# All high parts of g made by VectorE from PSUM, with w_y's parts ahead and w_out's and b_out's parts in the gate stage

## The chip, the cores and the metric

The kernel runs on one core of one Trainium2 chip, in one launch. The metric is the device time of that core in microseconds (us), the median of the runs that are shown. Each core has five engines that run side by side and meet only at semaphores: PE (TensorE, matrix multiply; its weight loads have a row of their own, PEld), DVE (VectorE), ACT (ScalarE), POOL (GpSimd) and SP (SyncE, here only the issuer of DMAs). Each takes its instructions strictly in the order in which the program wrote them. Matmuls read SBUF and write PSUM; DVE and ACT reach both; POOL works on SBUF alone.

## The reference

The input x has 2 sequences of 512 tokens and 256 channels. It is normalised per token (xn) and goes into two branches, whose outputs are added to x:

```
recurrent branch                                  feed-forward branch
y  = gelu(xn @ w_y + b_y)                         w1q, w3q, w2q = ternary(w) * mean|w|
conv = 4-tap causal conv of (xn @ w_x + b_x)      h1 = xn @ w1q.T ; h3 = xn @ w3q.T     (682 wide)
gate_x = sigmoid(conv @ w_ig + b_ig)              g  = silu(h1) * h3
gate_a = sigmoid(conv @ w_ag + b_ag)              out += g @ w2q.T
a  = exp(-8 gate_a softplus(a_param))
h_t = a_t h_(t-1) + gate_x conv sqrt(1 - a^2)     (a scan over the 512 tokens)
out += (h * y) @ w_out + b_out
```

All data is float32. The kernel multiplies in TensorE's rounded float32 type and keeps accuracy by splitting: an operand v becomes a high part (v rounded to that type) and a low part (v minus its high part), and a product of two such operands is three matmuls (high-high, high-low, low-high). A ternary weight is exact in the type, so a product with it needs only the two parts of the other operand.

## The kernel before

Channels lie on the 128 partitions, in KC = 2 chunks, and tokens along the free axis, 512 per sequence, so that nearly every elementwise instruction is 128x512. The order of work is written out by hand, engine by engine: the body of each `@block` is that engine's queue, and semaphores (`wait_ge`, `then_inc`) tie the queues together. PSUM is four slots of two banks, `slot[0]` to `slot[3]`, passed from stage to stage.

The stages, as PE sees them:

- **Start.** x is normalised on DVE (`statistics`, `variance`, `normalise`; the reciprocal root on POOL, `rstd_of`), transposed on PE, and split into `xt_hi` (ACT) and `xt_lo` (DVE). Weights are split too: `square_hi(m)` rounds one 256x256 matrix to `w_hi`, `square_lo(m)` makes `w_lo` on POOL. The matrices are WX, WY, WIG, WAG and WOUT.
- **Gate stage.** x @ w_x, x @ w_y, the convolution (`older_taps` on DVE), its parts `conv_hi` (ACT, L420) and `conv_lo` (POOL, `lo_of_conv`, L290), the products with w_ig and w_ag, then tanh and exp on ACT. `conv_lo(s, c)` of sequence s and chunk c is read by `gate_product` on PE. While this runs, DVE makes w1 and w3 ternary (`ternary_13`: two instructions `below`, L563, then two that write `w13_q`, L566) and after that w2 (`ternary_w2`, L604 and L606). PE's `sums_of_w13` has to be done before the first of these, and the first hidden tile needs both halves of `w13_q` and the scales that `threshold_2` makes (L571 to L576).
- **Hidden stage.** Ten tiles of 128 hidden channels by 512 tokens, `hidden(0)` to `hidden(9)`, eight matmuls each, put h1 into one bank and h3 into the other bank of one of slots 0 to 2. ACT makes `silu` of h1 (`silu_of`, L404); DVE multiplies by h3, which it reads from PSUM, into `g` (`g_of`, L616); ACT copies g into the high part `g_hi` (`g_hi_of`, L410; POOL does the last one, L329); POOL subtracts to the low part `g_lo` (`lo_of_g`, L295). silu and g have rings of three buffers. `hidden(n)` from n = 3 on waits until the g of the tile three before it has been made, since it uses that slot again. The last 42 channels go through `hidden_tail`, `tail_product` (L669), `tail_hi` and `tail_lo` (L676).
- **Scan and output.** `down(0)` and `down(1)` multiply g's parts with ternary w2, while the recurrence runs on the side: the square root on ACT (`mult_of`, L451, with a table load ahead of it), then on DVE `gated_products` (L638), `scan` (L649) and `gated_output` (L655) four times in a row, hy_hi on ACT (L457) and hy_lo on POOL (L346). `project(s, ...)` multiplies with w_out's parts (L812), and DVE adds x (`output`, L662). b_out rides in two extra rows of w2: its parts `b_split` are copied into `w2_q` by two small DMAs from SP, which wait for both.

In this kernel w_out's parts and b_split are made in the hidden stage: POOL waits for the squares of a (`a2_set`) and then makes both parts of w_out, ahead of its first `lo_of_g`; b_out's high part stands in ACT's queue after `g_hi_of(4)`, its low part in POOL's after the fifth `lo_of_g`. The two pads of the tail buffer gt (`gt_pads`, L286) stand between POOL's `lo_of_conv`.

## Time and profile before

| What | Value |
|---|---|
| three runs | 74.97, 74.77 and 74.32 us, median 74.77 |
| the profiled execution | 74.64 us, of which the profile's span covers 72.8 us |
| granted TensorE clock | 1.0 of full speed in every slice |
| PE busy | 68.1 us, 93% of the span |
| PEld busy | 58.9 us, 81% |
| DVE busy | 56.8 us, 78% |
| ACT busy | 52.5 us, 72% |
| POOL busy | 47.4 us, 65% |
| chain that ended last | PE 41%, DVE 17%, POOL 13%, issue 11%, ACT 9% of the span |

Busy shares are averages over stages that have different limits: a share tells which engine has much to do, not which one the end waits for. For that one reads, stage by stage, which wait ended last ahead of an instruction. Numbers on a time line are us from the start of the span. An instruction's row starts where its engine took it up; if it then had to wait for something that no semaphore shows, the wait is inside its duration, and it is seen by comparing with the same instruction elsewhere.

### The profile page before, as it was taken

The numbers are of one execution on the slowest core, as the hardware profiler recorded it, in microseconds if no ns is written. First come the engines' busy times: TensorE is split into PE (matmuls) and PEld (weight loads), VectorE is DVE, ScalarE is ACT, GpSimd is POOL, SyncE is SP. The second block draws the span as 40 slices with busy tenths as digits, with TensorE's granted clock in tenths as the row PEclk, the third lists the DMA queues.
The fourth block names the chain that finished last, engine by engine and source line by source line (L and its number), as shares of the span: only waits on it lengthen the run. The fifth ranks groups of instructions, "written<-read, shape, count | busy, mean of one in ns | idle before, by whom it ended". The sixth has DMA issues, their size and how long they took to land.

```text
span 72.8 us, 1128 instructions
## 1 busy us (share of the span) xinstructions
PE 68.1 (93%) x378; PEld 58.9 (81%) x378; DVE 56.8 (78%) x93; ACT 52.5 (72%) x81; POOL 47.4 (65%) x64
## 2 busy tenths in 40 slices
...
GB/s 6 230 295 332 361 377 395 382 99 0 9 0 0 4 0 0 0 0 0 0 0 9 0 0 9 0 0 0 1 0 0 0 0 0 9 0 0 200 193 183
DMA packets 5112, 5.63 MB, mean 77 GB/s; under 512 B 541, under 2 KB 4594, under 8 KB 5106
## 3 DMA queue, kind: packets, MB, share of 16 engines
...
## 4 chain that ended last, share of the span: by engine, by line
PE 41%; DVE 17%; POOL 13%; issue 11%; ACT 9%; DMA 3%; POOLq 2%; DVEq 0%; ACTq 0%
PE slot L753 21%; PE slot L770 10%; DVE slot L649 5%; PE slot L876 4%; DVE w_raw L616 4%; ACT w_raw L404 4%; POOL rstd L263 4%; DMA par<-params 3%; POOL w_lo L247 3%; PE slot L812 3%; PE slot L779 3%; DVE gt L676 2%; DVE xn_y L544 2%; DVE slot L638 2%; POOLq L52 2%
## 5 line engine op out<-in xcount | busy, mean ns | idle before, releaser
L295 POOL TENSOR_TENSOR g_lo<-w_raw,g_hi 128x512 fp32r<-128x512 f32 x10 | 14.7, 1488 | 2.3 <-ACT g_hi L410 2.2
L770 PE MATMUL slot<-xt_hi,w_q 128*128 128x512 f32 x40 | 15.8, 396 | 0.4 <-DVE w_raw L616 0.4
L770 PE MATMUL slot<-xt_lo,w_q 128*128 128x512 f32 x40 | 15.7, 393 | 0.0
L616 DVE SCALAR_TENSOR_TENSOR w_raw<-w_raw,s,slot 128x512 f32<-128x512 f32 x10 | 7.2, 746 | 5.2 <-ACT w_raw L404 5.2
L802 PE MATMUL slot<-w_q,g_lo 128*128 128x256 f32 x40 | 9.7, 283 | 0.0
L802 PE MATMUL slot<-w_q,g_hi 128*128 128x256 f32 x40 | 9.7, 283 | 0.0
L770 PEld LDWEIGHTS slot<-xt_hi,w_q 128*128 128x128 f32 x40 | 7.5, 188 | 2.6 <-DVE w_raw L616 1.0
L594 DVE SCALAR_TENSOR_TENSOR conv<-slot,par,conv 128x511 f32<-128x511 f32 (+2 forms) x12 | 9.0, 748 | 0.4
L770 PEld LDWEIGHTS slot<-xt_lo,w_q 128*128 128x128 f32 x40 | 7.5, 188 | 1.7
L242 POOL CAST w_hi<-w_raw 128x512 fp32r<-128x512 f32 x3 | 1.8, 614 | 9.7 <-DVE mult L628 9.7
L410 ACT ACTIVATE g_hi<-w_raw 128x512 fp32r<-128x512 f32 x9 | 5.7, 629 | 3.2 <-DVE w_raw L616 3.2
L802 PEld LDWEIGHTS slot<-w_q,g_lo 128*128 128x128 f32 x40 | 7.7, 192 | 0.0
L802 PEld LDWEIGHTS slot<-w_q,g_hi 128*128 128x128 f32 x40 | 7.7, 191 | 0.0
L247 POOL TENSOR_TENSOR w_lo<-w_raw,w_hi 128x512 fp32r<-128x512 f32 (+1 forms) x6 | 6.6, 1106 | 1.3 <-DVE xn_y L544 0.8
L404 ACT ACTIVATE w_raw<-slot,scale 128x512 f32<-128x512 f32 x10 | 6.6, 679 | 0.2
L346 POOL TENSOR_TENSOR conv_lo<-tx,conv_hi 128x512 fp32r<-128x512 f32 x4 | 5.1, 1284 | 2.3 <-ACT conv_hi L457 2.3
L819 PE MATMUL slot<-ones 128*128 128x128 f32 (+1 forms) x26 | 5.7, 408 | 1.0 <-POOL ones L230 1.0
L819 PEld LDWEIGHTS slot<-ones 128*128 128x128 f32 x26 | 5.5, 319 | 1.0 <-POOL ones L230 1.0
L457 ACT ACTIVATE conv_hi<-tx 128x512 fp32r<-128x512 f32 x4 | 2.5, 632 | 4.7 <-DVE tx L655 4.7
L290 POOL TENSOR_TENSOR conv_lo<-conv,conv_hi 128x512 fp32r<-128x512 f32 x4 | 5.7, 1420 | 0.2
L534 DVE BATCH_NORM_STATS2 stats<-x_sb 128x6 f32<-128x256 f32 x8 | 3.1, 413 | 2.3 <-DMA x_sb<-x 2.3
L753 PE MATMUL slot<-conv_hi,w_hi 128*128 128x512 f32 x12 | 4.7, 395 | 0.0
...
## 6 DMA issues: line engine op xcount, KB each, us to landing
...
```

Source lines behind the costliest of these rows:

```text
L247: nc.gpsimd.tensor_tensor(w_lo[:, m, c], w_raw[:, m, c], w_hi[:, m, c].bitcast(f32), ALU.subtract).then_inc(w_lo_set, len(chunks))
L290: nc.gpsimd.tensor_tensor(conv_lo[:, s, c], conv[:, s, c], conv_hi[:, s, c].bitcast(f32), ALU.subtract).then_inc(conv_lo_set, 1)
L295: nc.gpsimd.tensor_tensor(g_lo[:, j, s], g[:, n % RING], g_hi[:, j, s].bitcast(f32), ALU.subtract).then_inc(g_lo_set, 1)
L346: nc.gpsimd.tensor_tensor(hy_lo[:, s, c], tx[:, s, c], hy_hi[:, s, c].bitcast(f32), ALU.subtract).then_inc(hy_lo_set, 1)
L404: nc.scalar.activation(silu[:, n % RING], slot[H_SLOT[s][j]][:, 0], ACT.Silu, scale=scale[:, 0:1]).then_inc(silu_set, 1)
L410: nc.scalar.activation(g_hi[:, j, s], g[:, n % RING], ACT.Copy).then_inc(g_hi_set, 1)
L594: nc.vector.scalar_tensor_tensor(out=conv[:, s, c, i:], in0=slot[X_SLOT[s]][:, c, 0:SEQ - i], scalar=par[:, CONV_W + KC * k + c:CONV_W + K ...
L616: nc.vector.scalar_tensor_tensor(out=g[:, n % RING], in0=silu[:, n % RING], scalar=s32[:, 0:1], in1=slot[H_SLOT[s][j]][:, 1], op0=ALU.mult ...
L753: mm = nc.tensor.matmul(dst[:, o], w[:, m, c, o * P:(o + 1) * P], v[:, c], start=(first and i == 0 and c == 0), stop=(last and i == len(te ...
L770: mm = nc.tensor.matmul(slot[H_SLOT[s][j]][:, o], w13_q[:, c, col:col + P], v[:, s, c], start=(c == 0 and v is xt_hi), stop=(c == KC - 1 a ...
L802: nc.tensor.matmul(out_tile(s, i, t), v[:, s, rows], w2_q[:, j], start=(j == 0 and t == tiles.start and k == 0), stop=False, skip_group_ch ...
L819: nc.tensor.matmul(slot[WARM_SLOT][:, 0, 0:cols], ones[:, :], ones[:, 0:cols], start=True, stop=True)
```

## The change

Five edits go together.

- **g's high parts.** `g_hi_of(n)` moves from ACT (nine) and POOL (one) to DVE. It no longer rounds the stored g: it computes silu * s32 * h3 a second time from PSUM, with the output in the rounded type. It stands right behind `g_of(n)`. ACT's `silu_of` and PE's `hidden` now wait for `g_hi_set`, not `g_set`, since the second instruction reads the same buffers.
- **w_y.** ACT makes w_y's high part ahead of the Gelu table load; POOL makes the first half of its low part ahead of the second sequence's `rstd_of`. On PE, w_y's product is split so that the transposes of the second sequence stand between its terms, and on DVE one `statistics` of the second sequence stands between the two `xt_lo` of the first.
- **w_out.** Its high part goes to ACT behind `conv_hi_of(0, 0)`, its low part to POOL behind `lo_of_conv(0, 1)`, with semaphores of their own.
- **b_out.** The high part goes to ACT behind `gelu_of(0)`, the low part to POOL between `lo_of_conv(1, 0)` and `lo_of_conv(1, 1)`.
- **Pads and order.** One pad of gt goes to POOL's start, the other behind `lo_of_conv(0, 0)`. POOL's `half_biases` and `rates` come later. DVE's `gated_input(1)` moves from behind `g_of(1)` to ahead of `ternary_w2`, and `tail_lo` goes one tile later.

```diff
 POOL, at its start
+            nc.gpsimd.memset(gt[32:HALF].bitcast(f32), 1.0).then_inc(gt_pads_set, 1)
...
 POOL, start and gate stage
             square_lo(WX)
+            square_lo(WY, range(0, 1))
             rstd_of(1, slice(0, TILES // 2), 3)
             rstd_of(1, slice(TILES // 2, TILES), 4)
             pool.wait_ge(xn_set, 2 * TILES)
-            for c in range(KC):
-                square_lo(WY, range(c, c + 1))
+            square_lo(WY, range(1, KC))
             for m in (WIG, WAG):
                 square_hi(m)
                 square_lo(m)
             lo_of_conv(0, 0)
+            pool.wait_ge(conv_lo_set, 1)
+            nc.gpsimd.memset(gt[96:P].bitcast(f32), 0.0).then_inc(gt_pads_set, 1)
+            pool.wait_ge(gt_pads_set, 2)
+            lo_of_conv(0, 1)
+            pool.wait_ge(wout_hi_set, 1)
+            nc.gpsimd.tensor_tensor(w_lo[:, WOUT], w_raw[:, WOUT], w_hi[:, WOUT].bitcast(f32), ALU.subtract).then_inc(wout_lo_set, 1)
             half_biases()
             rates()
-            lo_of_conv(0, 1)
-            gt_pads(slice(32, HALF), 1.0, KC)
-            pool.wait_ge(gt_pads_set, 1)
             lo_of_conv(1, 0)
-            gt_pads(slice(96, P), 0.0, KC + 1)
-            pool.wait_ge(gt_pads_set, 2)
+            pool.wait_ge(b_hi_set, 1)
+            nc.gpsimd.tensor_tensor(b_split[:, 1], b_row[:, :], b_split[:, 0].bitcast(f32), ALU.subtract).then_inc(b_split_set, 1)
             lo_of_conv(1, 1)
-            pool.wait_ge(a2_set, SEQS)
-            square_hi(WOUT)
-            square_lo(WOUT)
             for n in range(2 * FULL):
-                if n == 2 * FULL - 1:
-                    pool.wait_ge(g_set, n + 1)
-                    nc.gpsimd.tensor_copy(g_hi[:, HJ[n][1], HJ[n][0]], g[:, n % RING]).then_inc(g_hi_set, 1)
                 lo_of_g(n)
...
 ACT
             xt_hi_of(0)
+            square_hi(WY)
             act.wait_ge(quarter_set, 2)
             nc.scalar.activation(gelu_in[:, 1:2], gelu_in[:, 0:1], ACT.Gelu)
-            square_hi(WY)
...
             conv_hi_of(0, 0)
+            act.wait_ge(w_loaded[WOUT], 16)
+            nc.scalar.activation(w_hi[:, WOUT], w_raw[:, WOUT], ACT.Copy).then_inc(wout_hi_set, 1)
             newest_tap(1)
             conv_hi_of(0, 1)
             gelu_of(0)
+            act.wait_ge(b_out_loaded, 16)
+            nc.scalar.activation(b_split[:, 0], b_row[:, :], ACT.Copy).then_inc(b_hi_set, 1)
...
-                    act.wait_ge(g_set, n - RING + 1)
+                    act.wait_ge(g_hi_set, n - RING + 1)
...
-            g_hi_of(0)
...
+            for n in range(2, 2 * FULL):
                 silu_of(n)
-                if n > FULL:
-                    g_hi_of(n - 1)
-                if n == FULL + 1:
+                if n == FULL - 1:
+                    tail_hi(gt_hi[HALF:HALF + TAIL])
+                if n == FULL + 2:
                     tail_hi(gt[0:TAIL])
...
 DVE
+            def g_hi_of(n):
+                s, j = HJ[n]
+                nc.vector.scalar_tensor_tensor(out=g_hi[:, j, s], in0=silu[:, n % RING], scalar=s32[:, 0:1],
+                                               in1=slot[H_SLOT[s][j]][:, 1], op0=ALU.mult, op1=ALU.mult).then_inc(g_hi_set, 1)
...
             gated_input(0)
+            gated_input(1)
             ternary_w2()
             squares(0)
             squares(1)
-            g_of(0)
-            g_of(1)
-            gated_input(1)
+            for n in range(2):
+                g_of(n)
+                g_hi_of(n)
             tail_product()
...
 PE
-            dense_terms(slot[Y_SLOT[0]], WY, [(w_hi, xt_hi[:, 0]), (w_hi, xt_lo[:, 0])], True, False)
+            dense_terms(slot[Y_SLOT[0]], WY, [(w_hi, xt_hi[:, 0])], True, False)
             transposes(1, first_half)
+            dense_terms(slot[Y_SLOT[0]], WY, [(w_hi, xt_lo[:, 0])], False, False)
             transposes(1, second_half)
...
             hidden(2)
-            pe.wait_ge(g_set, 1)
+            pe.wait_ge(g_hi_set, 1)
             hidden(3)
...
-            pe.wait_ge(w_lo_set, KC * (WOUT + 1))
+            pe.wait_ge(wout_lo_set, 1)
             project(0, range(len(O_TILES[0])))
```

POOL's queue in the gate stage, before (w_lo is a weight's low part, half_b to a_rate are the small constants, gt the tail's pads; the semaphores that an instruction waits for stand in brackets):

```order
L290 TENSOR_TENSOR conv_lo<-conv,conv_hi 128x512 [waits conv_hi_set]
L281 TENSOR_SCALAR half_b<-par 128x4
L252 TENSOR_SCALAR sp_e<-par 128x2 [waits sp_log]
L254 TENSOR_TENSOR sp_e<-sp_e 128x2 [waits rate_set]
L256 TENSOR_SCALAR a_rate<-sp_e 128x2 [waits rate_set]
L290 TENSOR_TENSOR conv_lo<-conv,conv_hi 128x512 [waits conv_hi_set]
L286 MEMSET gt 32x1024 [waits conv_lo_set]
L290 TENSOR_TENSOR conv_lo<-conv,conv_hi 128x512 [waits conv_hi_set,gt_pads_set]
L286 MEMSET gt 32x1024 [waits conv_lo_set]
L290 TENSOR_TENSOR conv_lo<-conv,conv_hi 128x512 [waits conv_hi_set,gt_pads_set]
L242 CAST w_hi<-w_raw 128x512 [waits w_loaded4,a2_set]
L247 TENSOR_TENSOR w_lo<-w_raw,w_hi 128x512 [waits w_hi_set]
```

The same stretch now:

```order
L293 TENSOR_TENSOR conv_lo<-conv,conv_hi 128x512 [waits conv_hi_set]
L318 MEMSET gt 32x1024 [waits conv_lo_set]
L293 TENSOR_TENSOR conv_lo<-conv,conv_hi 128x512 [waits conv_hi_set,gt_pads_set]
L322 TENSOR_TENSOR w_lo<-w_raw,w_hi 128x512 [waits wout_hi_set]
L289 TENSOR_SCALAR half_b<-par 128x4
L260 TENSOR_SCALAR sp_e<-par 128x2 [waits sp_log]
L262 TENSOR_TENSOR sp_e<-sp_e 128x2 [waits rate_set]
L264 TENSOR_SCALAR a_rate<-sp_e 128x2 [waits rate_set]
L293 TENSOR_TENSOR conv_lo<-conv,conv_hi 128x512 [waits conv_hi_set]
L327 TENSOR_TENSOR b_split<-b_row,b_split 1x256 [waits b_hi_set]
L293 TENSOR_TENSOR conv_lo<-conv,conv_hi 128x512 [waits conv_hi_set]
```

Between the second and the third conv_lo there are now w_out's low part and the four small instructions, where one pad stood; between the third and the fourth b_split stands in place of the other pad.

DVE's queue from the second sequence's gated input to the third g, before (tx is the gated input, mult the squares; w_raw with slot among its inputs is g, and with below the tail's product):

```order
L622 SCALAR_TENSOR_TENSOR tx<-tx,conv 128x1024 [waits tx_set]
L604 TENSOR_SCALAR below<-w_raw,thr 128x1536 [waits w13_q_set,s2_ready]
L606 SCALAR_TENSOR_TENSOR w_q<-w_raw,thr,below 128x1536 [waits below_set]
L628 TENSOR_TENSOR mult<-ta 128x2x511 [waits a_set] x2
L616 SCALAR_TENSOR_TENSOR w_raw<-w_raw,s,slot 128x512 [waits silu_set,scale2_set]
L616 SCALAR_TENSOR_TENSOR w_raw<-w_raw,s,slot 128x512 [waits silu_set]
L622 SCALAR_TENSOR_TENSOR tx<-tx,conv 128x1024 [waits tx_set]
L669 SCALAR_TENSOR_TENSOR w_raw<-below,s,slot 42x1024 [waits silu_t_set]
L616 SCALAR_TENSOR_TENSOR w_raw<-w_raw,s,slot 128x512 [waits silu_set]
```

The same stretch now:

```order
L612 SCALAR_TENSOR_TENSOR tx<-tx,conv 128x1024 [waits tx_set] x2
L588 TENSOR_SCALAR below<-w_raw,thr 128x1536 [waits w13_q_set,s2_ready]
L590 SCALAR_TENSOR_TENSOR w_q<-w_raw,thr,below 128x1536 [waits below_set]
L618 TENSOR_TENSOR mult<-ta 128x2x511 [waits a_set] x2
L600 SCALAR_TENSOR_TENSOR w_raw<-w_raw,s,slot 128x512 [waits silu_set,scale2_set]
L606 SCALAR_TENSOR_TENSOR g_hi<-w_raw,s,slot 128x512
L600 SCALAR_TENSOR_TENSOR w_raw<-w_raw,s,slot 128x512 [waits silu_set]
L606 SCALAR_TENSOR_TENSOR g_hi<-w_raw,s,slot 128x512
L659 SCALAR_TENSOR_TENSOR w_raw<-below,s,slot 42x1024 [waits silu_t_set]
L600 SCALAR_TENSOR_TENSOR w_raw<-w_raw,s,slot 128x512 [waits silu_set]
L606 SCALAR_TENSOR_TENSOR g_hi<-w_raw,s,slot 128x512
```

Both gated inputs stand ahead of the first g, and each g is followed by its g_hi, so that the first g_hi is the seventh instruction behind the first gated input.

## Rows read from the trace of the kernel before

**Rows 1.** Time line, PE: start, duration, engine, line, operation, out<-in, shape, count, idle time before.

```profile
32.10 0.39 PE L770 MATMUL slot<-xt_hi,w_q 128*128 128x512 f32 x1
...
39.49 0.39 PE L770 MATMUL slot<-xt_hi,w_q 128*128 128x512 f32 x1
...
49.30 0.50 PE L770 MATMUL slot<-xt_hi,w_q 128*128 128x512 f32 x1 [0.39 <-DVE w_raw L616]
...
53.10 0.28 PE L802 MATMUL slot<-w_q,g_hi 128*128 128x256 f32 x1
...
67.44 0.40 PE L812 MATMUL slot<-w_lo,conv_hi 128*128 128x256 f32 x2
```

**Rows 2.** The chain of waits, its end: start, duration, what.

```profile
68.30 1.94 PE slot L812 x14
```

**Rows 3.** Time line, POOL: the last low part of hy.

```profile
66.97 1.27 POOL L346 TENSOR_TENSOR conv_lo<-tx,conv_hi 128x512 fp32r<-128x512 f32 x1 [0.64 <-ACT conv_hi L457]
```

**Rows 4.** Time line, DVE: the first gated product.

```profile
56.94 0.70 DVE L638 TENSOR_TENSOR slot<-tx,slot 128x512 f32<-128x512 f32 x1 [1.19 <-ACT slot L451]
```

**Rows 5.** Time line, ACT: the last silu.

```profile
54.16 0.67 ACT L404 ACTIVATE w_raw<-slot,scale 128x512 f32<-128x512 f32 x1
```

**Rows 6.** Time line, DVE, from 24 us to the tail.

```profile
24.14 2.77 DVE L563 TENSOR_SCALAR below<-w_raw,thr 128x1408 bf16<-128x1408 f32 x2
...
31.47 1.21 DVE L622 SCALAR_TENSOR_TENSOR tx<-tx,conv 128x1024 f32<-128x1024 f32 x1
32.60 1.01 DVE L604 TENSOR_SCALAR below<-w_raw,thr 128x1536 bf16<-128x1536 f32 x1
...
37.65 1.41 DVE L616 SCALAR_TENSOR_TENSOR w_raw<-w_raw,s,slot 128x512 f32<-128x512 f32 x2
38.96 1.97 DVE L622 SCALAR_TENSOR_TENSOR tx<-tx,conv 128x1024 f32<-128x1024 f32 x1
40.97 1.29 DVE L669 SCALAR_TENSOR_TENSOR w_raw<-below,s,slot 42x1024 f32<-42x1024 f32 x1
...
46.31 2.16 DVE L676 TENSOR_TENSOR gt<-w_raw,gt_hi 42x1024 fp32r<-42x1024 f32 x1
```

**Rows 7.** Groups by line and shape, DVE's ternary instructions: busy us, mean ns, idle before.

```profile
L566 DVE SCALAR_TENSOR_TENSOR w_q<-w_raw,thr,below 128x1408 fp32r<-128x1408 f32 x1 | 2.7, 2705 | 0.0
L563 DVE TENSOR_SCALAR below<-w_raw,thr 128x1364 bf16<-128x1364 f32 x1 | 1.7, 1698 | 0.0
L566 DVE SCALAR_TENSOR_TENSOR w_q<-w_raw,thr,below 128x1364 fp32r<-128x1364 f32 x1 | 1.6, 1627 | 0.0
L563 DVE TENSOR_SCALAR below<-w_raw,thr 128x1408 bf16<-128x1408 f32 x1 | 1.1, 1146 | 0.0
```

**Rows 8.** Time line, ACT: the last tap and conv_hi(0, 1) in the gate stage.

```profile
18.05 1.44 ACT L389 ACTIVATE conv<-slot,conv_c,par 128x509 f32<-128x509 f32 x2 [0.62 <-PE slot L753]
19.38 0.63 ACT L420 ACTIVATE conv_hi<-conv 128x512 fp32r<-128x512 f32 x1
```

**Rows 9.** Time line, POOL, the second rstd and the gate stage.

```profile
10.12 0.22 POOL L260 TENSOR_SCALAR v_eps<-mv 128x2 f32<-128x2 f32 x1 [1.40 <-DVE mv L539]
...
19.76 0.24 POOL L281 TENSOR_SCALAR half_b<-par 128x4 f32<-128x4 f32 x1
...
20.86 1.30 POOL L290 TENSOR_TENSOR conv_lo<-conv,conv_hi 128x512 fp32r<-128x512 f32 x1
22.22 0.95 POOL L286 MEMSET gt<- 32x1024 f32 x1
23.25 1.29 POOL L290 TENSOR_TENSOR conv_lo<-conv,conv_hi 128x512 fp32r<-128x512 f32 x1
24.60 1.58 POOL L286 MEMSET gt<- 32x1024 f32 x1
26.26 1.79 POOL L290 TENSOR_TENSOR conv_lo<-conv,conv_hi 128x512 fp32r<-128x512 f32 x1
```

**Rows 10.** Groups by line and shape, POOL: b_out's low part.

```profile
L333 POOL TENSOR_TENSOR b_split<-b_row,b_split 1x256 fp32r<-1x256 f32 x1 | 0.7, 728 | 0.0
```

More of the change, by code:

```diff
@@ L182, in build @@
         o_psum, o_set = sem("o_psum"), sem("o_set")
+        LAST = 2 * FULL - 2
         HJ = [(s, j) for s in range(SEQS) for j in range(FULL)]
@@ L402, in silu_of @@
                 if n >= RING:
-                    act.wait_ge(g_set, n - RING + 1)
+                    act.wait_ge(g_hi_set, n - RING + 1)
                 nc.scalar.activation(silu[:, n % RING], slot[H_SLOT[s][j]][:, 0], ACT.Silu,
                                      scale=scale[:, 0:1]).then_inc(silu_set, 1)
-            def g_hi_of(n):
-                s, j = HJ[n]
-                act.wait_ge(g_set, n + 1)
-                nc.scalar.activation(g_hi[:, j, s], g[:, n % RING], ACT.Copy).then_inc(g_hi_set, 1)
             def tail_hi(dst):
@@ L494, in _ @@
                                  scale=scale[0:TAIL, 0:1]).then_inc(silu_t_set, 1)
-            g_hi_of(1)
-            silu_of(2)
-            silu_of(3)
-            g_hi_of(2)
-            tail_hi(gt_hi[HALF:HALF + TAIL])
-            silu_of(4)
-            g_hi_of(3)
-            g_hi_of(4)
-            act.wait_ge(b_out_loaded, 16)
-            nc.scalar.activation(b_split[:, 0], b_row[:, :], ACT.Copy).then_inc(b_hi_set, 1)
-            for n in range(FULL, 2 * FULL - 1):
+            for n in range(2, 2 * FULL):
                 silu_of(n)
-                if n > FULL:
-                    g_hi_of(n - 1)
-                if n == FULL + 1:
+                if n == FULL - 1:
+                    tail_hi(gt_hi[HALF:HALF + TAIL])
+                if n == FULL + 2:
                     tail_hi(gt[0:TAIL])
-            g_hi_of(2 * FULL - 2)
-            silu_of(2 * FULL - 1)
             for s in range(SEQS):
@@ L545, in normalise, with xt_lo_of @@
                                             ALU.subtract, ALU.mult).then_inc(xn_set, 1)
-            def xt_lo_of(s):
-                for h in range(2):
+            def xt_lo_of(s, parts=range(2)):
+                for h in parts:
                     dve.wait_ge(xt_hi_set, 2 * s + h + 1)
@@ L687, in _ @@
                 normalise(0, tile_halves[i], i + 1)
-            xt_lo_of(0)
-            for i in range(2):
-                dve.wait_ge(x_loaded[TILES + i], 16)
-                statistics(1, tile_halves[i])
-                variance(1, tile_halves[i])
+            xt_lo_of(0, [0])
+            dve.wait_ge(x_loaded[TILES], 16)
+            statistics(1, [0])
+            xt_lo_of(0, [1])
+            statistics(1, [1])
+            variance(1, tile_halves[0])
+            dve.wait_ge(x_loaded[TILES + 1], 16)
+            statistics(1, tile_halves[1])
+            variance(1, tile_halves[1])
             normalise(1, tile_halves[0], 3)
@@ L709, in _ @@
             squares(1)
-            g_of(0)
-            g_of(1)
-            gated_input(1)
+            for n in range(2):
+                g_of(n)
+                g_hi_of(n)
             tail_product()
-            g_of(2)
-            g_of(3)
-            g_of(4)
-            tail_lo()
-            for n in range(FULL, 2 * FULL - 1):
-                g_of(n)
-            dve.wait_ge(g_set, 9)
-            first_root(0, 0)
-            g_of(9)
-            dve.wait_ge(g_set, 10)
-            first_root(0, 1)
+            for n in range(2, LAST):
+                g_of(n)
+                g_hi_of(n)
+                if n == FULL:
+                    tail_lo()
+            for n in range(LAST, 2 * FULL):
+                g_of(n)
+                g_hi_of(n)
+                dve.wait_ge(g_hi_set, n + 1)
+                first_root(0, n - LAST)
             for s in range(SEQS):
```

36 lines of the change are left out of this document (18 added, 18 removed).

## The prediction, made before the changed kernel was run

> **What bounds the kernel now.** I read the engines' busy shares, then the chain of waits from its end, then the time lines of the engines it runs through, stage by stage. The profiled execution took 74.64 us, 0.13 under the median of the runs (74.77); all sums are made against it.
>
> The chain's last step is 1.94 us of PE from 68.30 [rows 2], and that start is where two strands meet. One is PE itself. Its hidden stage runs from 32.10 to 53.10 at (39.49 - 32.10) / 4 = 1.85 us per tile of eight matmuls (the tail's eight count as a tile), 0.23 each, with one wait ahead of hidden(8) [rows 1]: that starts at 49.30 where 1.85 a tile allows 39.49 + 5 x 1.85 = 48.74, and its first matmul takes 0.50 instead of 0.39, so about 0.65 is lost there. From 53.10, which I call H, PE goes without a gap until the two matmuls at 67.44, which at 0.12 each free it at 67.68 [rows 1]: 14.58 us from H. The other strand begins with the last silu, silu(9), at 54.16 [rows 5], goes through the root to DVE's first gated product, which waited 1.19 for ACT [rows 4], and through scans, hy_hi and hy_lo to 66.97 + 1.27 = 68.24 [rows 3]. That is 14.08 from silu(9). PE stands 0.62 waiting for it. So H may rise by 0.6 before PE alone is late, provided that silu(9) does not rise too; it starts 1.06 behind H now, because ACT's copies of g stand ahead of it, and a hand-over needs only about 0.22 (a matmul's row lasts 0.39 and the next starts after 0.23, so 0.16, and 0.06 from hy_lo's end to PE's start) [rows 1 to 3, 5].
>
> Ahead of the hidden stage DVE is the engine to watch. From 24.14 to 31.08 it makes w1 and w3 ternary [rows 6], while POOL works at conv_lo and pads [rows 9]. There the same instruction takes very different times [rows 7]. `below` on w2, undisturbed, takes 1.01 for 1536 elements [rows 6], so 0.93 and 0.90 are due for 1408 and 1364; it took 1146 and 1698 ns. w_q took 1627 ns for 1364, so 1.68 is due for 1408; it took 2705 ns. Losses: 0.2, 0.8 and 1.0. In the same stretch POOL's second pad took 1.58 instead of 0.95 and the last conv_lo 1.79 instead of 1.29 [rows 9]. The two engines take turns here.
>
> **The change, part by part.** *POOL's gate stage.* conv_lo(0, 1) cannot start before conv_hi(0, 1) ends at 19.38 + 0.63 = 20.0 [rows 8]. Then follow 1.30 for it, 1.30 for w_out's low part (priced by conv_lo, the same subtraction and shape) and 1.10 for half_biases and rates (20.86 - 19.76): conv_lo(1, 0) starts at 23.7 where it started at 23.25, and ends at 25.0 [rows 9]. DVE, ready at about 24.1 [rows 6], stands until then. After that the turns are 0.93 `below`, 0.73 b_split [rows 10], 0.90 `below`, 1.29 conv_lo(1, 1), 1.68 and 1.63 w_q: 25.0 + 7.16 = 32.2. Neighbouring rows of an engine overlap by 0.08 (24.14 + 2.77 against 26.83 [rows 6]), 0.4 over five joints, so 31.8, against 31.08: +0.7.
>
> The unknown is b_split, on one partition. No row shows such an instruction in DVE's way, so it costs DVE between 0 and 0.73. I take 0.73, because the nearest row, a pad on 32 of 128 partitions, cost `below` the 0.8 above. By the Trainium skill ("SBUF — State Buffer", section "Who interferes with whom") the engine that issues first holds the shared ports for its whole instruction and the other one fully blocks; by that, width does not count, the 0.73 stands and the result is the forecast's, while without it DVE would be 0.73 earlier and the second rival below would hold.
>
> *DVE up to the first g_hi.* Before, g(0) starts at 37.65 [rows 6]. Now it comes 0.7 later, and another 1.13 later for gated_input(1), which is moved ahead of it (32.60 - 31.47): 39.5. g and g_hi are 0.70 each (1.41 for two), so g_hi(0) ends at 40.9 [rows 6]. g_hi is priced as g, from which it differs only in its output type.
>
> *PE up to hidden(3).* hidden(0) needs DVE's scales, which end 0.4 behind w13_q [rows 6], at 32.1 or 32.2, and it needs the gate products, whose last 14 matmuls at 0.23 follow conv_lo(1, 1) at about 28.8: 32.0. So it starts where it did, at 32.1, whatever w_y's new place gains PE before. hidden(3), ready at 39.49, now waits for g_hi(0) until 40.95: +1.45 on PE.
>
> *The rest of the hidden stage.* A pair costs DVE 1.4 against PE's 1.85 per tile, so DVE catches up. tail_product (1.29 [rows 6]) stands between the second and third pair: g_hi(2) ends at 40.9 + 1.4 + 1.3 + 1.4 less joints, 44.85, where hidden(5) is ready at 40.95 + 2 x 1.85 = 44.65: +0.25. The 0.65 lost ahead of hidden(8) had tail_lo (2.16 at 46.31 [rows 6]) ahead of g(5); that now stands behind g_hi(5), which ends at 48.9, with hidden(8) ready at 50.45: -0.65. tail_lo then ends at 51.1 at its old length, g_hi(6) at 52.4, and hidden(9) is ready at 52.3: +0.1. H = 53.10 + 1.45 + 0.25 - 0.65 + 0.1 = 54.25.
>
> *The end.* PE frees itself at 54.25 + 14.58 = 68.83. silu(9) has no copies ahead of it and starts at H + 0.22 = 54.47, so hy_lo ends at 68.55, and PE no longer waits for it. 68.83 instead of 68.30 is 0.53, less 0.1 for a first matmul that no longer follows a wait: +0.45. Result 74.64 + 0.45 = 75.1.
>
> *At nothing.* ACT loses nine copies and POOL two casts and one subtraction in the hidden stage; neither is late there but for silu(9), already counted. The first pad at POOL's start lies in its wait for the parameters, and the half of w_y's low part, 0.7, in the 1.40 that it is idle at 10.12 [rows 9]. w_out's high part on ACT, 0.63 like conv_hi, fits the idle 0.62 ahead of the last tap [rows 8]; were that gone, conv_hi(0, 1) and all of POOL's stretch would come 0.6 later, which is the first rival's case. b_out's high part stands ahead of conv_hi(1, 0), with POOL's use of it at 23.7, two microseconds later. SP's two b_split DMAs come earlier and have only stores behind them. On PE's start the transposes move between w_y's terms; what that gains ends at the wait for the scales.
>
> **Rivals.** *POOL comes too late (slower).* If POOL reaches conv_lo(1, 0) after DVE has begun `below`, about 24.0, the turns change: `below` to 24.95, conv_lo(1, 0) to 26.25, `below`, b_split to 27.9, w_q to 29.6, and only then conv_lo(1, 1), to 30.9. The gate products then let hidden(0) start at about 34.1, hidden(3) at 41.5, and H is 54.8: +1.0, 75.6. It decides at a delay of 0.3 on POOL between 20.0 and 23.7; for it speaks that POOL waits for ACT twice there, against it that w_out's high part is done long before. Chance 0.22.
>
> *b_split does not hold DVE (faster).* DVE is 0.73 earlier from the first `below` on, hidden(3) waits 0.7, H is 53.5, silu(9)'s strand ends at 67.8 and PE at 68.1: -0.3, 74.3. Is POOL also 0.4 quicker up to conv_lo(1, 0) than summed, and hence DVE, it is 73.9. For it speaks that one partition is little, against it the pad's 1.58 and DVE's 1698 ns [rows 7, 9]. Chance 0.25.
>
> *DVE becomes the bound of the hidden stage.* If g_hi costs more than g, or tail_lo and the pairs are disturbed by POOL's g_lo, H slips by 0.5 more: 75.6. Against it: 1.4 against 1.85 a tile. Chance 0.08.
>
> **How the numbers follow.** The forecast, 75.1, has 0.45; its own range is 74.7 to 75.5, from the joints and hand-overs that I rounded. The range of 73.9 to 75.8 takes in the first two rivals but for their outer ends. One per cent, 0.75 us, is about what a measurement of this kernel can tell from no change. Faster than 74.0 takes the better half of the second rival and a tenth for what I have not seen, mostly at PE's start: 0.22. Slower than 75.5 takes most of the first, the third and a tenth of the forecast: 0.27. Within: 0.51.
>
> **What would show it.** A wait of DVE's about 0.9 inside the first `below` (some 1.8 instead of 1146 ns), a second `below` of about 1.6 and a first w_q of 2.9; PE waiting 1.4 for g_hi ahead of hidden(3) and not ahead of hidden(8); silu(9) within 0.3 of H; no wait of PE's for hy_lo at the end. I am wrong if conv_lo(1, 1) ends past 30, if hidden(3) starts before 40.3, or if PE's last wait is still for hy_lo.

## The result, and the profile of the changed kernel

| Timing | before | changed | ratio (95% interval) |
|---|---|---|---|
| first, 4 runs each | 74.56 us | 75.38 us | 1.0096 (1.0058 to 1.0134) |
| again, 12 runs beside 23 of before | 74.67 us | 74.97 us | 1.0046 (1.0026 to 1.0066) |

The changed kernel is slower, by 0.8 us in the first timing and by 0.3 us in the second. The forecast was 75.1, +0.45. Executions of one kernel also differ ahead of the gate stage: DVE's first `below` starts at 24.38 and at 23.98 in two profiles of the changed kernel, and at 24.14 before [rows 6]. So the profiles are compared from this start on, and in the changed kernel the rows are those of the execution with 24.38. From there PE's last matmuls end 46.10 later before (68.30 + 1.94 [rows 2]) and 46.52 later now: **+0.42**. The rows follow; each answers to rows of before.

Time line of DVE in the changed kernel, from w13's ternary instructions to the tail:

```profile
24.38 4.38 DVE L547 TENSOR_SCALAR below<-w_raw,thr 128x1408 bf16<-128x1408 f32 x2
28.68 3.22 DVE L550 SCALAR_TENSOR_TENSOR w_q<-w_raw,thr,below 128x1408 fp32r<-128x1408 f32 x2
...
32.28 2.35 DVE L612 SCALAR_TENSOR_TENSOR tx<-tx,conv 128x1024 f32<-128x1024 f32 x2
...
39.60 0.74 DVE L600 SCALAR_TENSOR_TENSOR w_raw<-w_raw,s,slot 128x512 f32<-128x512 f32 x1
40.26 0.74 DVE L606 SCALAR_TENSOR_TENSOR g_hi<-w_raw,s,slot 128x512 fp32r<-128x512 f32 x1
...
41.58 0.74 DVE L606 SCALAR_TENSOR_TENSOR g_hi<-w_raw,s,slot 128x512 fp32r<-128x512 f32 x1
...
44.33 0.74 DVE L606 SCALAR_TENSOR_TENSOR g_hi<-w_raw,s,slot 128x512 fp32r<-128x512 f32 x1
...
49.44 1.22 DVE L666 TENSOR_TENSOR gt<-w_raw,gt_hi 42x1024 fp32r<-42x1024 f32 x1
```

The first g_hi ends at 41.00 (forecast 40.9). Three things put it there, and all are in the rows: w1 and w3 are ternary at 31.90, 7.52 after the first `below`, where it was 6.94 [rows 6]; two gated inputs stand ahead of w2 (2.35) where one stood (1.21); and g_hi itself takes 0.66 from start to start, as g does, so it was priced right.

Time line of PE, at hidden(0), hidden(3), hidden(5) and H (the first matmul of the down stage):

```profile
32.44 0.47 PE L764 MATMUL slot<-xt_hi,w_q 128*128 128x512 f32 x1 [0.24 <-DVE thr L557]
...
41.05 0.50 PE L764 MATMUL slot<-xt_hi,w_q 128*128 128x512 f32 x1 [0.99 <-DVE g_hi L606]
...
45.13 0.50 PE L764 MATMUL slot<-xt_hi,w_q 128*128 128x512 f32 x1
...
54.49 0.28 PE L796 MATMUL slot<-w_q,g_hi 128*128 128x256 f32 x1
```

The wait ahead of hidden(8) [rows 1] is gone, and one ahead of hidden(3) is there. A small one stands at hidden(5), which starts 0.28 after the 44.85 that the tile before it allows; the view does not mark it. H is 30.11 after the first `below`, before it was 28.96: +1.15, as the terms of the forecast sum to.

The chain of waits of the changed kernel, its end (start, duration, what):

```profile
45.13 9.52 PE slot L764 x40
54.65 10.54 PE slot L796 x88
65.19 5.71 PE slot L806 x48
70.93 0.42 DVE x_sb L652
```

From hidden(5) on the chain is PE alone: no wait for hy_lo, which stood at 68.30 before [rows 2]. ACT's last silu and POOL's last hy_lo, from their time lines:

```profile
54.69 0.69 ACT L402 ACTIVATE w_raw<-slot,scale 128x512 f32<-128x512 f32 x1 [1.16 <-PE slot L764]
```

```profile
67.51 1.30 POOL L344 TENSOR_TENSOR conv_lo<-tx,conv_hi 128x512 fp32r<-128x512 f32 x1 [0.64 <-ACT conv_hi L450]
```

The last silu is 0.20 behind H (before 1.06 [rows 1, 5]); hy_lo ends at 68.81, 0.26 ahead of the matmul that reads it (54.49 + 14.58 = 69.07). The 0.6 that PE used to wait at the end paid for half of the later H.

Time line of POOL, from the start to the hidden stage, and DVE's ternary groups (busy us, mean ns):

```profile
9.57 0.74 POOL L255 TENSOR_TENSOR w_lo<-w_raw,w_hi 128x256 fp32r<-128x256 f32 x1 [1.04 <-ACT w_hi L353]
...
19.33 0.95 POOL L318 MEMSET gt<- 32x1024 f32 x1
20.39 1.29 POOL L293 TENSOR_TENSOR conv_lo<-conv,conv_hi 128x512 fp32r<-128x512 f32 x1
21.65 1.29 POOL L322 TENSOR_TENSOR w_lo<-w_raw,w_hi 128x512 fp32r<-128x512 f32 x1
23.02 0.25 POOL L289 TENSOR_SCALAR half_b<-par 128x4 f32<-128x4 f32 x1
...
24.14 1.30 POOL L293 TENSOR_TENSOR conv_lo<-conv,conv_hi 128x512 fp32r<-128x512 f32 x1
25.38 1.39 POOL L327 TENSOR_TENSOR b_split<-b_row,b_split 1x256 fp32r<-1x256 f32 x1
26.74 1.29 POOL L293 TENSOR_TENSOR conv_lo<-conv,conv_hi 128x512 fp32r<-128x512 f32 x1
41.08 2.62 POOL L298 TENSOR_TENSOR g_lo<-w_raw,g_hi 128x512 fp32r<-128x512 f32 x2 [13.05 <-DVE g_hi L606]
...
49.49 2.33 POOL L298 TENSOR_TENSOR g_lo<-w_raw,g_hi 128x512 fp32r<-128x512 f32 x1 [0.40 <-DVE g_hi L606]
```

```profile
L547 DVE TENSOR_SCALAR below<-w_raw,thr 128x1364 bf16<-128x1364 f32 x1 | 2.7, 2655 | 0.0
...
L547 DVE TENSOR_SCALAR below<-w_raw,thr 128x1408 bf16<-128x1408 f32 x1 | 1.8, 1802 | 0.0
L550 DVE SCALAR_TENSOR_TENSOR w_q<-w_raw,thr,below 128x1408 fp32r<-128x1408 f32 x1 | 1.7, 1672 | 0.0
```

Against the undisturbed times, 0.93 and 0.90, DVE lost 0.87 in the first `below` and 1.75 in the second, 2.6 in all (before 2.0 [rows 7]). conv_lo(1, 0) came 0.24 ahead of the first `below`: that narrow was the margin. In the hidden stage g_hi takes its 0.74 also beside POOL's g_lo (41.58, while two g_lo run from 41.08 to 43.70), and tail_lo, taken up at 49.44, comes 0.05 ahead of a g_lo: here it is POOL that loses, 2.33 for 1.3.

### The profile page after: what moved, and what is told of

It is laid out like the page before. It is cut to its first block, busy times and chain, and to the rows that moved or that the text cites. A ratio compares the mean times of both kernels' runs of the same rounds, so it can differ in the third digit from the quotient of the medians.

```text
span 73.6 us, 1128 instructions
## 1 busy us (share of the span) xinstructions
PE 68.4 (93%) x378; PEld 59.0 (80%) x378; DVE 62.0 (84%) x103; ACT 48.2 (66%) x73; POOL 44.9 (61%) x62
## 4 chain that ended last, share of the span: by engine, by line
PE 48%; DVE 38%; issue 8%; ACT 2%; POOL 0%; DVEq 0%; ACTq 0%; POOLq 0%
PE slot L796 14%; PE slot L764 13%; DVE conv L578 10%; PE slot L806 8%; PE slot L813 7%; DVE below L547 6%; PE slot L838 4%; DVE mult L618 3%; DVE tx L612 3%; DVE g_hi L606 3%; DVE w_q L550 2%; DVE w_raw L600 2%; DVE w_q L590 2%; DVE xt_lo L534 2%; DVE below L588 1%
## 5 line engine op out<-in xcount | busy, mean ns | idle before, releaser
L298 POOL TENSOR_TENSOR g_lo<-w_raw,g_hi 128x512 fp32r<-128x512 f32 x10 | 14.0, 1401 | 16.2 <-DVE g_hi L606 16.1
L606 DVE SCALAR_TENSOR_TENSOR g_hi<-w_raw,s,slot 128x512 fp32r<-128x512 f32 x10 | 7.4, 742 | 0.0
L255 POOL TENSOR_TENSOR w_lo<-w_raw,w_hi 128x512 fp32r<-128x512 f32 (+1 forms) x5 | 5.4, 1071 | 2.4 <-ACT w_hi L353 1.0
L293 POOL TENSOR_TENSOR conv_lo<-conv,conv_hi 128x512 fp32r<-128x512 f32 x4 | 5.2, 1291 | 0.2
L747 PE MATMUL slot<-conv_hi,w_lo 128*128 128x512 f32 x12 | 4.7, 393 | 0.0
```

The source lines that it names most:

```text
L255: nc.gpsimd.tensor_tensor(w_lo[:, m, c], w_raw[:, m, c], w_hi[:, m, c].bitcast(f32), ALU.subtract).then_inc(w_lo_set, len(chunks))
L293: nc.gpsimd.tensor_tensor(conv_lo[:, s, c], conv[:, s, c], conv_hi[:, s, c].bitcast(f32), ALU.subtract).then_inc(conv_lo_set, 1)
L298: nc.gpsimd.tensor_tensor(g_lo[:, j, s], g[:, n % RING], g_hi[:, j, s].bitcast(f32), ALU.subtract).then_inc(g_lo_set, 1)
L606: nc.vector.scalar_tensor_tensor(out=g_hi[:, j, s], in0=silu[:, n % RING], scalar=s32[:, 0:1], in1=slot[H_SLOT[s][j]][:, 1], op0=ALU.mult, ...
L747: mm = nc.tensor.matmul(dst[:, o], w[:, m, c, o * P:(o + 1) * P], v[:, c], start=(first and i == 0 and c == 0), stop=(last and i == len(te ...
```

## The experiments

The theory: what was lost is lateness in DVE's queue up to the third g_hi, made of turns that POOL takes, of gated_input(1) and of the pairs of g and g_hi; PE is late by what they are late. Rivals: the ten pairs set the hidden stage's end whatever stands ahead; b_split does not hold DVE; the start is to blame. Every ratio below is against runs of the kernel before, taken beside it. The new places of the two pads were not tried by themselves.

**The changed kernel again**, unaltered, as the measure for the others:

> The changed kernel once more, unaltered, as a measure for the others of this group: its first timing rests on four runs (ratio 1.0096, 1.0058 to 1.0134), and the profiles of the variants start up to 0.3 us apart, by when x arrives. All theories: 1.006 to 1.012.

Measured 1.0046 (1.0026 to 1.0066), just under what all theories gave, with an interval that reaches into it. Its profile has the same waits, 0.4 earlier throughout: from the first `below` on, H (30.11) and PE's end (46.52) are the same to the hundredth. The kernels below are set beside this second timing. Expectations written ahead of it went by the first, 1.0096, and so lie about 0.005 too high.

**b_out's low part back in the loop of g_lo.**

```diff
 lo_of_conv(1, 0)
-b_split on POOL
 lo_of_conv(1, 1)
 for n in range(2 * FULL):
     lo_of_g(n)
+    if n == FULL - 1: b_split on POOL
```

> The changed kernel with one thing undone: b_out's low part (b_split on POOL, one partition) stands behind the fifth lo_of_g again, no longer between the last two lo_of_conv. Theory (all that is lost is lateness of DVE's queue up to the first g_hi, and PE is late by the same amount): the second 'below' took 2655 ns beside b_split and conv_lo; without b_split's 0.73 it takes about 1.9, the first g_hi ends 0.7 earlier (40.3 for 41.0), hidden(3) starts at 40.3, the hidden stage ends at 53.8 for 54.49, and the time falls by 0.7, to that of the kernel before (ratio 1.000). Rival A (ten pairs of g and g_hi on DVE set the hidden stage's end, whatever stands ahead): hidden(3) starts earlier, but later tiles wait and the time stays at ratio 1.009. Rival B (one partition does not hold DVE): the second 'below' keeps its 2.6 us, because conv_lo comes at once.

Measured 1.0099 (1.0064 to 1.0134): the gain did not come, but not for the reason that rival A has. Time lines of this kernel, DVE, PE and POOL:

```profile
24.30 3.67 DVE L548 TENSOR_SCALAR below<-w_raw,thr 128x1408 bf16<-128x1408 f32 x2
...
48.65 2.67 DVE L667 TENSOR_TENSOR gt<-w_raw,gt_hi 42x1024 fp32r<-42x1024 f32 x1
```

```profile
40.27 0.51 PE L765 MATMUL slot<-xt_hi,w_q 128*128 128x512 f32 x1 [0.76 <-DVE g_hi L607]
52.81 0.50 PE L765 MATMUL slot<-xt_hi,w_q 128*128 128x512 f32 x1 [0.80 <-DVE g_hi L607]
```

```profile
48.25 0.73 POOL L331 TENSOR_TENSOR b_split<-b_row,b_split 1x256 fp32r<-1x256 f32 x1
48.95 1.28 POOL L298 TENSOR_TENSOR g_lo<-w_raw,g_hi 128x512 fp32r<-128x512 f32 x1
```

The two `below` took 3.67 for 4.38, so b_split had cost DVE 0.71 of its 0.73, on one partition: rival B falls. hidden(3) started 0.78 earlier (0.70 counted from the first `below`). In its new place b_split stood beside tail_lo, which asked at 48.65, was kept out by b_split and by g_lo(5) behind it, and took 2.67 for 1.22; hidden(9) then waited 0.80. The loss had moved, and it had grown: H is 30.46 after the first `below`, for 30.11 in the changed kernel.

**w_out's low part behind the squares.**

```diff
 lo_of_conv(0, 1)
-pool.wait_ge(wout_hi_set, 1); w_out's low part
 half_biases(); rates()
 lo_of_conv(1, 0); b_split; lo_of_conv(1, 1)
+pool.wait_ge(a2_set, SEQS); pool.wait_ge(wout_hi_set, 1); w_out's low part
```

> The changed kernel with w_out's low part on POOL behind the last lo_of_conv, where it waits for the squares of a (about 39.7 us) instead of standing ahead of half_biases. Theory (DVE's queue): POOL reaches conv_lo(1, 0) 1.3 earlier, at 22.8 for 24.14, so it is over before DVE's first 'below' (24.38). b_split then holds that 'below' for about 0.5 in place of the 0.87 lost now, and conv_lo(1, 1), which waits for conv_hi(1, 1) until 25.3, holds the second for 1.2 in place of 1.75. The first g_hi ends about 0.9 earlier, the time falls by 0.9: ratio 0.998. w_out's low part then runs beside g and g_hi, which read PSUM, and disturbs nothing. Rival A (the pairs): ratio stays 1.009. Rival C (each conflict avoided comes back with the next instruction of POOL): the first g_hi ends less than 0.3 earlier.

Measured 0.9879 (0.9858 to 0.9900), 1.7% below the changed kernel's second timing, more than expected. DVE's groups of this kernel:

```profile
L548 DVE TENSOR_SCALAR below<-w_raw,thr 128x1364 bf16<-128x1364 f32 x1 | 2.0, 1965 | 0.0
...
L548 DVE TENSOR_SCALAR below<-w_raw,thr 128x1408 bf16<-128x1408 f32 x1 | 1.2, 1244 | 0.0
```

The two `below` lost 0.31 and 1.06, 1.37 for 2.62: 1.25 less, where I had counted 0.9. PE's last matmuls end 45.27 after the first `below`, for 46.52: 1.25 less, too, and the time fell by as much (1.67% of 74.77). What DVE gained there arrived in full at the end.

**gated_input(1), in two other places.**

```diff
-gated_input(0); gated_input(1); ternary_w2()
+gated_input(0); ternary_w2()
 ...
+gated_input(1)      # first kernel: behind the second pair; second kernel: behind the seventh
```

> The changed kernel with gated_input(1) behind the second pair of g and g_hi, where the kernel before has it, instead of ahead of w2's ternary instructions. Theory: the first g_hi ends 1.13 earlier, at 39.9, and hidden(3) starts at 39.95 for 41.05; but gated_input(1) and the tail's product now both stand ahead of the third pair, g_hi(2) ends at 45.1 as it does now, hidden(5), ready at 43.6, waits 1.4, and the time is unchanged: ratio 1.009, between 1.006 and 1.012. Rival (only the first g_hi counts): the time falls by 1.0, ratio 0.996.

Measured 1.0036 (1.0018 to 1.0055), unchanged within the intervals. hidden(3) did not wait; PE's wait stood two tiles later, and PE ends 46.54 after the first `below`, for 46.52. Time lines of DVE, gated_input(1), and of PE:

```profile
40.92 1.22 DVE L612 SCALAR_TENSOR_TENSOR tx<-tx,conv 128x1024 f32<-128x1024 f32 x1
```

```profile
44.96 0.50 PE L764 MATMUL slot<-xt_hi,w_q 128*128 128x512 f32 x1 [1.26 <-DVE g_hi L606]
```

> The changed kernel with gated_input(1) behind the seventh pair of g and g_hi, the last one that PE's hidden tiles wait for. Theory: the first g_hi ends at 39.9, hidden(3) starts there, hidden(5) waits 0.3 (tail's product ahead of its pair), nothing else does; the hidden stage ends at about 53.5 for 54.49, and the time falls by 1.0 to 74.3 where before has 74.56: ratio 0.997. gated_input(1) delays the last three pairs by 1.2 to 2.0, which end by 57 or 58, when the first gated product starts (57.5 now): up to 0.5 of the gain may be lost there if POOL's g_lo and it disturb one another. Rival A (the pairs set the end): hidden(6) to hidden(9) each wait and the ratio stays at 1.009.

Measured 0.9976 (0.9949 to 1.0003). H came 1.1 earlier (53.38), and no hidden tile from hidden(6) on waited: rival A, the pairs as the bound, falls. PE then waited for hy_lo:

```profile
68.45 0.50 PE L807 MATMUL slot<-w_hi,conv_lo 128*128 128x256 f32 x2 [0.33 <-POOL conv_lo L344]
```

The last pairs, and with them the first gated product, came later against H (57.09, which is 3.71 behind it; 2.99 in the changed kernel): part of the gain was lost where expected, so that, counted from the first `below`, PE ends 0.57 earlier where H is 1.16 earlier.

**Both low parts behind the squares.**

```diff
-w_out's low part ahead of half_biases; b_split behind lo_of_conv(1, 0)
+lo_of_conv(1, 1); pool.wait_ge(a2_set, SEQS); w_out's low part; b_split
```

> The changed kernel with both low parts on POOL, w_out's and b_out's, behind the squares of a (38 us), where DVE goes on to g and g_hi, which read PSUM. Theory (POOL's turns ahead of w13's ternary instructions are what was lost): both 'below' of the stretch lose only conv_lo(1, 1)'s turn, 1.0 to 1.3; the first g_hi ends at 39.0, hidden(3) waits for nothing, nor does hidden(5), the hidden stage ends at about 52.5, PE alone sets the time: ratio 0.983 (e2_wlo_late had 0.988). Rival (b_split costs something wherever it stands, as behind lo_of_g(4)): g_lo(0) starts 0.7 later, a DVE instruction behind it is blocked, ratio 0.988 or more.

Measured 0.9874 (0.9838 to 0.9910), which does not tell the two expectations apart and is no better than w_out's part alone. Of what b_split takes, only the 0.31 lost in the first `below` above was left to win, since conv_lo(1, 1) waits for its high part on ACT and takes its turn from DVE anyway. This is argued from the rows above; an interval of 0.3 us to either side cannot show it.

**The high parts of g alone, and all but them.**

```diff
 first kernel: the changed kernel, with g_hi as before
-g_hi_of(n) on DVE behind g_of(n)
+g_hi_of(n) on ACT (the last on POOL)
 second kernel: the kernel before, with this edit alone
-g_hi_of(n) on ACT (the last on POOL)
+g_hi_of(n) on DVE behind g_of(n); tail_lo behind the sixth pair
```

> The changed kernel with the high parts of g back on ACT (the last one on POOL), all else as changed. Theory: DVE reaches g(0) as late as in the changed kernel, hidden(3) waits for g(0) alone and starts at 40.4 for 41.05, the hidden stage ends at 53.5 to 53.7 for 54.49; the last silu is 1.06 behind it again because of ACT's copies, hy_lo ends at 68.7 and PE waits for it; ratio 1.004 (1.002 to 1.007). Rival A (the pairs on DVE are the whole loss): 1.000 or less. Rival B (g's high parts cost nothing, start and gate stage are the whole loss): as the changed kernel, 1.009.

Measured 0.9992 (0.9963 to 1.0021), below the range that I gave the theory. hidden(3) started at 40.39 and H was 53.73, both as expected. What I had wrong is the last silu: it came at 54.43, 0.70 behind H and not 1.06, which is 30.05 after the first `below` (24.38) where it was 30.02 before [rows 5, 6]. So hy_lo ended at 68.52 and not at 68.7, no later than before (44.14 after the first `below`, for 44.10), and PE's later H went into the wait for it.

> The kernel before with the high parts of g on DVE as the only edit (gated_input(1) stays behind the second pair, tail_lo goes behind the sixth; w_y's, w_out's and b_out's parts stay). Theory: the first g_hi ends at 39.1, hidden(3) does not wait; gated_input(1) and tail_product delay g_hi(2) to 44.2 to 44.9, hidden(5), ready at 43.2, waits 1.0 to 1.7; the loss ahead of hidden(8) goes; the hidden stage ends at 53.5 to 54.1, the last silu right behind it: ratio 1.000 (0.998 to 1.005). Rival A (the pairs are the whole loss of the changed kernel): 1.009. Rival B (on its own the move is a gain, since ACT's copies no longer stand ahead of the last silu): 0.992 or less.

Measured 1.0199 (1.0175 to 1.0223): far above what any of the three expectations had. PE's waits of this kernel, and DVE's gated_input(1) and tail_lo:

```profile
45.04 0.50 PE L757 MATMUL slot<-xt_hi,w_q 128*128 128x512 f32 x1 [1.70 <-DVE g_hi L603]
53.52 0.50 PE L757 MATMUL slot<-xt_hi,w_q 128*128 128x512 f32 x1 [0.81 <-DVE g_hi L603]
```

```profile
40.32 1.90 DVE L609 SCALAR_TENSOR_TENSOR tx<-tx,conv 128x1024 f32<-128x1024 f32 x1
...
49.35 2.67 DVE L663 TENSOR_TENSOR gt<-w_raw,gt_hi 42x1024 fp32r<-42x1024 f32 x1
```

hidden(5) waited 1.7, as expected at the upper end; hidden(9)'s 0.81 is b_split beside tail_lo again. The two parts of the change are not additive: g's high parts cost 2.0% on the kernel before and 0.5% with the rest, and the rest, worth nothing alone, takes 1.5% off them. It does so by clearing POOL's work from beside gated_input(1) and tail_lo. The kernel with gated_input(1) behind the second pair (1.0036) shows this: the DVE order from g(0) on is the same, but gated_input(1) takes 1.22 for 1.90, hidden(5) waits 1.26 for 1.70 and hidden(9) not at all. That is 1.25 less waiting, or 1.7%, and the times differ by 1.6%.

**b_out's low part out of the loop, in that last kernel.**

```diff
 w_out's low part
+b_split on POOL        # b_out's high part on ACT behind gelu_of(0)
 for n in range(2 * FULL):
     lo_of_g(n)
-    if n == FULL - 1: b_split on POOL
```

> e7_ghi_only (the kernel before, with g's high parts on DVE alone, ratio 1.020) with b_out's low part taken out of the loop of lo_of_g and put behind w_out's low part ahead of it; its high part goes on ACT behind the first Gelu. In e7 POOL's b_split and g_lo(5) stood one behind the other and tail_lo took 2.67 for 1.22; hidden(9) lost 0.9. Theory: tail_lo falls to about 1.25, the loss ahead of hidden(9) goes, the time falls by 0.7 to 1.0: ratio 1.007 to 1.011. Rival (tail_lo is disturbed by g_lo(5) whatever stands ahead of it): tail_lo 2 or more, ratio 1.015 to 1.020.

Measured 1.0581 (1.0528 to 1.0634). tail_lo fell to 1.22 and hidden(9)'s wait went, as the theory has it, but something larger took their place. Time lines of POOL, DVE and PE, and the stretches behind (start:end, length, then busy time and count of PE, PEld, DVE, ACT and POOL, granted clock, DMA's share and GB/s):

```profile
39.76 0.73 POOL L327 TENSOR_TENSOR b_split<-b_row,b_split 1x256 fp32r<-1x256 f32 x1
40.46 2.53 POOL L295 TENSOR_TENSOR g_lo<-w_raw,g_hi 128x512 fp32r<-128x512 f32 x2
```

```profile
40.23 3.84 DVE L608 SCALAR_TENSOR_TENSOR tx<-tx,conv 128x1024 f32<-128x1024 f32 x1
```

```profile
46.88 0.79 PE L756 MATMUL slot<-xt_hi,w_q 128*128 128x512 f32 x1 [3.62 <-DVE g_hi L602]
```

```profile
40.00:45.00 5.00, 3.27 (x15) 2.32 (x13) 4.97 (x3) 1.69 (x3) 2.99 (x3) 1.00 0.01 0
45.00:50.00 5.00, 3.12 (x7) 2.48 (x8) 4.43 (x7) 1.05 (x1) 3.02 (x3) 0.52 0.01 3
50.00:55.00 5.00, 5.00 (x19) 4.02 (x18) 3.51 (x5) 1.38 (x2) 2.92 (x2) 0.80 0.00 0
```

gated_input(1) asked at 40.23 during b_split and was kept out until two g_lo had run, too, at 42.99: 3.84 for 1.21. hidden(5) waited 3.62, until 46.88. From 45 to 50 us the granted clock was 0.52, nearly all at the lower of its two levels (1.2 of 2.4 GHz), and then 0.80. From hidden(5) to H PE took 11.70 (46.88 to 58.58), where the changed kernel, also without a wait, took 9.36 (45.13 to 54.49): 2.34 for the clock. Wait and clock come to 5.96. Most of the rest, down to the 4.85 us above before (79.58 for 74.73), is what before itself lost ahead of hidden(8) and for hy_lo, 0.65 and 0.62 [rows 1, 2].

**w_out's part late and gated_input(1) behind the fifth pair.**

```diff
 the kernel with w_out's low part behind the squares, and on DVE:
-gated_input(1) ahead of ternary_w2(); tail_lo() behind the sixth pair
+gated_input(1) behind the fifth pair; tail_lo() behind the seventh
```

> e2_wlo_late (w_out's low part behind the squares) with gated_input(1) behind the fifth pair and tail_lo behind the seventh, on DVE. In e2_wlo_late PE still lost 0.24 ahead of hidden(0), 0.46 ahead of hidden(3) and 0.38 ahead of hidden(5). Theory: with gated_input(1) out of the way, g_hi(0) ends 1.13 earlier and the last two losses go, hidden(9) may lose up to 0.3; the time falls by 0.5 to 0.8 below e2's: ratio 0.978 to 0.982. Rival (e2 already stands on another bound, the strand over hy_lo or PE's own work): 0.986 to 0.990, with a wait for hy_lo at the end.

Measured 0.9764 (0.9733 to 0.9794), 72.91 us, a little under the range expected: the best version, ahead of both kernels. No hidden tile waits; H is at 52.07, 27.99 after the first `below` (30.11 in the changed kernel, 28.85 with w_out's low part late alone).

**A semaphore between b_split and conv_lo.**

```diff
 b_split on POOL
+pool.wait_ge(b_split_set, 1)
 lo_of_conv(1, 1)
```

> The changed kernel with one semaphore wait more on POOL, between b_split and the last lo_of_conv (it waits for b_split's own end). In the changed kernel the second 'below', ready at 26.1, waited for both b_split and conv_lo(1, 1), 2655 ns in all, and the first w_q then ran undisturbed (1672 ns). Theory (POOL instructions that follow one another without a semaphore keep the shared ports, a waiting DVE instruction gets in only where POOL stops for one): the second 'below' gets in behind b_split and takes about 1.65, conv_lo(1, 1) follows and ends 1.0 later, the first w_q waits for it and takes about 2.7 to 3.0; the sum, and so the first g_hi and the time, stay or grow by up to 0.3: ratio 1.004 to 1.010. Rival (who gets in depends on the instant at which each asks, not on the semaphore): the second 'below' keeps 2.65 us and w_q 1.67.

Measured 1.0056 (1.0036 to 1.0077). DVE's groups:

```profile
L551 DVE SCALAR_TENSOR_TENSOR w_q<-w_raw,thr,below 128x1408 fp32r<-128x1408 f32 x1 | 2.7, 2708 | 0.0
...
L548 DVE TENSOR_SCALAR below<-w_raw,thr 128x1364 bf16<-128x1364 f32 x1 | 1.4, 1403 | 0.0
```

The second `below` got in ahead of conv_lo(1, 1) (1403 for 2655 ns) and the first w_q paid instead (2708 for 1672): the order of turns that I had forecast for the changed kernel, at the same time within the intervals. In the trace the two `below` and the two w_q together took 0.21 less (7.54 for 7.76), which the timings do not resolve. The rule behind it is only half shown, though: in the changed kernel itself the first `below` got in between conv_lo(1, 0) and b_split, where POOL waits for ACT's b_hi_set, long met, and not for work of its own.

**w_y's edits undone.**

```diff
-POOL: square_lo(WY, range(0, 1)) ahead of rstd_of(1, ...)
+POOL: both halves of w_y's low part behind rstd_of(1, ...)
-ACT: square_hi(WY) ahead of the Gelu table load
+ACT: square_hi(WY) behind it
 and DVE's statistics and PE's terms of w_y in the old order
```

> The changed kernel with w_y's edits undone: ACT makes its high part behind the Gelu table load, POOL both halves of its low part behind the second sequence's rstd, PE's product and DVE's statistics in the old order. Theory: the start was worth nothing, since PE waits for the scales ahead of hidden(0) anyway (0.24 idle); but in the changed kernel conv_hi(0, 1) and all that POOL does behind it came 0.2 to 0.4 later than in the kernel before; if w_y's new place does that, the time falls by 0.2 to 0.4, ratio 0.999 to 1.003, and if w_out's high part on ACT does it, the ratio stays at 1.005. Rival (the start gained something that the other edits lost): 1.008 or more.

Measured 1.0075 (1.0058 to 1.0092): no gain, and above the changed kernel's second timing. Time lines of POOL and PE:

```profile
24.12 0.96 POOL L264 TENSOR_SCALAR a_rate<-sp_e 128x2 f32<-128x2 f32 x1
25.16 1.83 POOL L293 TENSOR_TENSOR conv_lo<-conv,conv_hi 128x512 fp32r<-128x512 f32 x1
26.95 2.12 POOL L327 TENSOR_TENSOR b_split<-b_row,b_split 1x256 fp32r<-1x256 f32 x1
29.03 1.25 POOL L293 TENSOR_TENSOR conv_lo<-conv,conv_hi 128x512 fp32r<-128x512 f32 x1
```

```profile
30.34 0.72 PE L743 MATMUL slot<-conv_lo,w_hi 128*128 128x512 f32 x2 [1.45 <-POOL conv_lo L293]
```

This is the prediction's first rival in the flesh: POOL came to a_rate at 24.12, when DVE's `below` had just begun (24.04); both `below` then ran undisturbed (956 and 926 ns), POOL's rest slipped behind them, conv_lo(1, 1) ended at 30.3 and PE waited 1.45 for it. What w_y's edits do is to bring POOL there in time: with them conv_lo(1, 0) starts 0.24 ahead of the first `below`, and here it started behind a_rate, which took 0.96 for 0.23, at 25.16.

## Why the prediction was right, step by step

- **POOL's gate stage.** conv_lo(1, 0) was to run from 23.7 to 25.0 ahead of DVE's first `below`; it ran from 24.14 to 25.44. Of the 0.44, 0.24 is conv_hi(0, 1), which ended at 20.25 and is as late as the first `below`. Most of the rest lies ahead of conv_lo(0, 1), which started at 20.39: the sum had it wait for conv_hi(0, 1) alone, and it also waits for the pad, which ended at 20.28. The order held by 0.24 where the sum had 0.4. That it held is in part luck, as the kernel without w_y's edits shows.
- **DVE's losses.** +0.7 forecast; from the first `below`, +0.58. Right in sum, wrong in order, and two of the signs that the prediction named did not come: I had one POOL instruction per turn of DVE's, so a second `below` of 1.6 and a first w_q of 2.9; measured 2655 and 1672 ns.
- **b_split.** The forecast took its full 0.73, out of 0 to 0.73; it cost 0.71. So the second rival is refuted. The Trainium skill ("SBUF — State Buffer", section "Who interferes with whom") states that the shared ports are held for the whole instruction. The traces agree, with 0.71 lost to an instruction on one partition.
- **The hidden stage.** hidden(3) +1.45 forecast, 41.05 - 39.49 - 0.24 = +1.32 measured (the wait itself is 1.14, from the 39.91 at which the tile was ready, since hidden(0) started at 32.44 and not at 32.1); hidden(5) +0.25 and measured 0.28; the first matmuls of these two, which follow a wait, 0.11 more each; hidden(8) -0.65, and its wait is gone; hidden(9) +0.1, and measured none, since tail_lo took 1.22 there and not 2.16. H +1.15, measured +1.15. The terms are right to within 0.15; that their sum is right to the hundredth is luck.
- **The end.** Last silu at H + 0.22, measured 0.20; no wait for hy_lo; +0.45, measured +0.42 in the profile, between the +0.30 and +0.82 of the two timings.
- **The start, costed at nothing.** It was no gain for PE, as said, which waits 0.24 for the scales ahead of hidden(0), but it was not worth nothing: without w_y's edits the first rival comes true. That rival was priced at +1.0 (75.6) and measured 1.0075, about +0.6: hidden(0) started at 33.70 and hidden(3) at 41.09, for 34.1 and 41.5.
- **The third rival** (DVE the bound of the hidden stage) did not come true in the changed kernel, but its mechanism, tail_lo disturbed by POOL, did in the two kernels that leave b_split in the loop of g_lo.

One thing stays open: by what rule a waiting DVE instruction gets in between two of POOL's. One that asked during a 128x512 subtraction got in before the next one (the first `below` in the changed kernel, gated_input(1) with 1.90 where g's high parts moved alone). One that asked during b_split was kept out until POOL had to wait for a semaphore, in eight kernels: the second `below` in the changed kernel and three others, tail_lo in two, gated_input(1) in one, and the second w_q in the one without w_y's edits. No run here tells why.
